# VectorE sums four experts in place of two, and the output projection is issued in halves

## What is computed

```python
y = jnp.moveaxis(ys, 0, 1) + D[None, None, :, None] * xh       # the scan's result, 384 wide
y = y.reshape(B, L, D_INNER) * jax.nn.silu(z)
h = y @ out_proj_w                                             # the output projection
v = _rmsnorm(h, norm2_w)
m = jax.nn.silu(v @ w_gate) * (v @ w_up) @ w_down
...
h1 = jnp.einsum('td,eid->tei', x2, w1)                         # 8 experts, x2 normed
h3 = jnp.einsum('td,eid->tei', x2, w3)
h = jax.nn.silu(h1) * h3
y = jnp.einsum('tei,edi,te->td', h, w2, cw)                    # cw: the routing weights
z = jax.nn.silu(x2 @ sw1.T) * (x2 @ sw3.T) @ sw2.T             # the shared expert
return (y + z).reshape(B, S, D)
```

## Time and profile before

| | us |
|---|---|
| median of 3 runs | 1014.93 (1013.69 to 1015.32) |
| profiled execution, its own time | 1016.41 |
| its span in the trace | 1014.4 |
| busy PE / PEld / DVE / ACT / POOL | 825.3 / 637.8 / 660.8 / 585.1 / 345.4 |
| share of the span | 81 / 63 / 65 / 58 / 34 % |

### The profile page before, as it was taken

The page is one execution under the profiler, slowest core; times in us unless marked ns, Lnnn a source line. Parts: engine busy times, 40 slices in busy tenths (PEclk is TensorE's granted clock), DMA queues, the critical chain, the costliest instruction groups (busy, mean ns, idle before and its releaser), DMA issues.

```text
span 1014.4 us, 22717 instructions
## 1 busy us (share of the span) xinstructions
PE 825.3 (81%) x7120; PEld 637.8 (63%) x7120; DVE 660.8 (65%) x1629; ACT 585.1 (58%) x1307; POOL 345.4 (34%) x508
## 2 busy tenths in 40 slices
PE   3363898888888888888888888888888888888867
PEld 2232676666667666666767666666766666676656
DVE  5565675757667685766768575766768576665524
ACT  3574565665656666665656566565666666565423
POOL 1222333343324344333433334332434433242402
PEclk9675999999999999999999999999999999999988
DMA  8200000000000000000000000000000000000000
GB/s 221 81 1 12 2 6 15 2 20 0 19 0 5 14 0 19 0 19 0 5 14 4 15 0 19 0 20 0 5 14 0 19 0 19 0 5 9 1 8 8
DMA packets 16466, 15.22 MB, mean 15 GB/s; under 512 B 6322, under 2 KB 15224, under 8 KB 16184
## 3 DMA queue, kind: packets, MB, share of 16 engines
q1 hardware_dynamic: 16440, 14.89, 5.5%
HBM read 10.69 MB, written 4.19 MB: 15 GB/s over the span
## 4 chain that ended last, share of the span: by engine, by line
PE 42%; DVE 23%; issue 16%; ACT 13%; POOL 3%; DVEq 1%; ACTq 1%; DMA 0%; POOLq 0%; SPq 0%
PE bank L1305 20%; DVE mr L1024 5%; DVE xa L966 4%; PE bank L1471 4%; PE bank L1513 3%; PE bank L1588 3%; PE bank L1537 3%; DVE w_raw L1188 2%; ACT L687 2%; ACT xk L651 2%; ACT L812 2%; ACT er L706 2%; DVE e_ge L1117 2%; POOL t L476 1%; PE bank L1450 1%
## 5 line engine op out<-in xcount | busy, mean ns | idle before, releaser
L1024 DVE SCALAR_TENSOR_TENSOR mr<-er,gm 128x512 f32<-128x512 f32 x192 | 129.2, 702 | 58.1 <-ACT er L706 57.7
L540 POOL TENSOR_TENSOR w_raw<-w_raw 128x384 f32<-128x384 f32 x96 | 99.2, 1034 | 145.9 <-ACT w_raw L767 143.6
L778 ACT ACTIVATE sg<-bank 128x256 f32<-128x256 f32 x144 | 55.3, 384 | 136.2 <-PE bank L1305 135.9
L1588 PE MATMUL bank<-w2t,w_raw 128*128 128x192 f32 x576 | 116.4, 329 | 7.4 <-ACT w_raw L767 7.4
L706 ACT ACTIVATE er<-bank 128x512 f32<-128x512 f32 x192 | 104.3, 597 | 30.4 <-PE bank L1450 29.9
L1471 PE MATMUL bank<-mr,xd 128*32 128x128 f32 x1536 | 90.9, 288 | 28.0 <-DVE mr L1024 26.6
L966 DVE SCALAR_TENSOR_TENSOR xa<-xr,cw_,xa 128x256 f32<-128x256 f32 x192 | 101.4, 536 | 4.4 <-ACT xa L617 0.4
L1305 PE MATMUL bank<-x_h,w_hi 128*128 128x256 f16 x288 | 79.9, 277 | 29.6 <-DVE w_raw L1188 27.5
L1188 DVE TENSOR_TENSOR w_raw<-sg,bank 128x256 f32<-128x256 f32 x144 | 60.3, 420 | 61.5 <-ACT sg L778 56.3
L1588 PEld LDWEIGHTS bank<-w2t,w_raw 128*128 128x128 f32 x576 | 90.5, 190 | 13.3 <-ACT w_raw L767 9.6
L737 ACT ACTIVATE sg<-bank 128x256 f32<-128x256 f32 x96 | 36.9, 384 | 105.2 <-PE bank L1305 104.8
(11 more groups left out here) (233 smaller groups left out, 2160.4 us busy)
## 6 DMA issues: line engine op xcount, KB each, us to landing
out<-w_raw SPq DMA_DIRECT2D x16, 192.0 KB, 2.0
w_raw<-weights SPq DMA_DIRECT2D x1, 1924.0 KB, 9.6
wt_raw<-weights SPq DMA_DIRECT2D x2, 962.0 KB, 14.9
pos<-position SPq DMA_DIRECT2D x16, 96.0 KB, 2.8
tok<-tokens SPq DMA_DIRECT2D x16, 70.0 KB
sums<-lj SPq DMA_DIRECT2D x16, 64.0 KB, 2.2
ri<-sums SPq DMA_DIRECT2D x64, 12.0 KB
w2t<-w SPq DMA_DIRECT2D x1, 864.0 KB, 19.7
```

Of the source, the lines that this page charges most:

```text
L540: pool.tensor_tensor(acc[:], acc[:], wt_out[:, e % NWT], ALU.add).then_inc(acc_done, 1)
L778: act.activation(sg[:, e % 2, :], p_pair[e % 2][:, 0:NB * Q], ACT.Silu).then_inc(sx_ready, 1)
L1024: ve.scalar_tensor_tensor(mr[:, r % NER], er[:, r % NER], 1.0, gm[:, b, :].unsqueeze(1).to_broadcast([128, HG, Q]), ALU.min, ALU.mult)\
L1588: ins = pe.matmul(p_out[(e + 1) % 2][:, b * D:(b + 1) * D], hh[:, e % NHH, b * Q:(b + 1) * Q], w2t[:, e, :], start=True, stop=True)
```

## The change

1. `NP` becomes 5 and `ND = NX - NP` is 4. ScalarE no longer weighs experts 5 and 6, GpSimd no longer adds them, VectorE's `weighed_sum` takes 5, 6, 7 and 8. The sum of expert 5 stands ahead of the product `hh` of expert 8 in VectorE's queue, the others behind it. TensorE's `down(7)` and `down(8)` wait for `out_sum`, no longer for `weighed`.
2. `project_out` is called once for each batch row; the exponents of unit 2 are issued between the two calls and those of unit 3 behind the second. In `scan` they are left out. The waits for `y_ready` are split likewise.
3. ScalarE's `mixed` comes ahead of the Exp of unit 3, not of unit 2.

```diff
-        NP = NX - 2
+        NP = NX - 4
+        ND = NX - NP
...
-                    for out_ in {2: (0,), 8: (5, 6)}.get(e, (e - 3,) if e > 3 else ()):
+                    for out_ in {2: (0,), 8: ()}.get(e, (e - 3,) if e > 3 else ()):
...
-                    scan(f, 0, {} if b is None else {2: lambda: mixed(b), 4: lambda: mixed_norm(b)})
+                    scan(f, 0, {} if b is None else {3: lambda: mixed(b), 4: lambda: mixed_norm(b)})
...
                 for e in range(NX):
+                    if e == NX - 1:
+                        weighed_sum(c, NP)
                     ve.wait_ge(sx_ready, c * NX + e + 1)
...
-                for e in range(NP, NX):
+                for e in range(NP + 1, NX):
                     weighed_sum(c, e)
...
-                    ve.wait_ge(out_sum, c * 2 + e - NP)
+                    ve.wait_ge(out_sum, c * ND + e - NP)
...
-                        if b * NQ + q + 2 < NR:
+                        if 3 < b * NQ + q + 2 < NR:
                             exponents(c, b * NQ + q + 2)
...
-            def project_out(c):
-                if not later(c):
-                    pe.wait_ge(in_late, 96)
-                    pe.wait_ge(dx_ready, 2)
-                pe.wait_ge(y_ready[0], c + 1)
-                pe.wait_ge(y_ready[1], c + 1)
-                if later(c):
-
-                    pe.wait_ge(out_sum, c * 2 - 1)
-                for b in range(NB):
-                    for k in range(DI // 128):
-                        ins = pe.matmul(p_out[0][:, b * D:(b + 1) * D], y[:, b, k, :], wo[:, k, :],
-                                        start=(k == 0), stop=(k == DI // 128 - 1))
-                ins.then_inc(m_out, 1)
+            def project_out(c, b):
+                if b == 0:
+                    if not later(c):
+                        pe.wait_ge(in_late, 96)
+                        pe.wait_ge(dx_ready, 2)
+                    if later(c):
+
+                        pe.wait_ge(out_sum, c * ND - 1)
+                pe.wait_ge(y_ready[b], c + 1)
+                for k in range(DI // 128):
+                    ins = pe.matmul(p_out[0][:, b * D:(b + 1) * D], y[:, b, k, :], wo[:, k, :],
+                                    start=(k == 0), stop=(k == DI // 128 - 1))
+                if b == NB - 1:
+                    ins.then_inc(m_out, 1)
...
-                        pe.wait_ge(weighed, c * NP + e - 1)
+                        if e - 2 < NP:
+                            pe.wait_ge(weighed, c * NP + e - 1)
+                        else:
+                            pe.wait_ge(out_sum, c * ND + e - 1 - NP)
...
-                    project_out(b)
+                    project_out(b, 0)
+                if f is not None:
+                    exponents(f, 2)
+                if b is not None:
+                    project_out(b, 1)
+                if f is not None:
+                    exponents(f, 3)
```

More of the change, by code:

```diff
@@ L382, in store @@
             def store(c):
-                sp.wait_ge(out_sum, c * 2 + 2)
+                sp.wait_ge(out_sum, c * ND + ND)
                 settle(sp)
@@ L1519, in turn_v @@
                 if later(c):
-                    pe.wait_ge(out_sum, c * 2)
+                    pe.wait_ge(out_sum, c * ND)
                 transpose_channels(p_out[1], vn, vt_done)
```

## The result

| | before | after |
|---|---|---|
| median | 1015.12 us (4 runs, 1013.69 to 1015.45) | 999.73 us (4 runs, 998.91 to 1004.04) |
| profiled execution, its span | 1016.41, 1014.4 | 999.18, 997.4 |
| mean granted TensorE clock | 0.962 | 0.959 |
| level pass (whole pass at granted clock 1.00) | 57.95 | 56.80 |

The changed kernel takes 0.986 of the time before, with an interval of 0.983 to 0.989: **15.4 us less**. The forecast was 1001.7 us, with a range of 993.3 to 1007.0.

What follows compares the result with a forecast made beforehand. No engine was taken as full: waits bound the kernel, at the boundary ScalarE's chain. 14 x 0.83 = 11.6, + 1.0 + 0.9 - 0.3 = 13.2 us off 1016.41, less 1.48 to the median: 1001.7 us, range 993.3 to 1007.

Steps and rivals of the forecast that it cites:

- Exponents 0, 1.09 us earlier: At the boundary between two bodies: without ScalarE's four weighings, TensorE starts exponents 0 1.09 us earlier, between 0.81 and 1.25.
- both legs nearly even: Ahead of exponents 0: TensorE, through VectorE's sums and `down(8)`, is free 0.1 us after ScalarE's `ecx`.
- VectorE's three steps: Ahead of `down(8)`: sum of expert 5 (0.76 us), `hh` of expert 8 (0.42), sum of expert 6 (0.76).
- the loop's branch: On TensorE, between `down(8)` and exponents 0: taken as 0.05 us, with bounds of nothing and 0.28.
- The projection in halves, 0.26 us: Exponents 2 ahead of the projection's second half makes the projection end 0.26 us later, counted from exponents 0.
- GpSimd in the way: In the scan: `decayed` starts 0.11 us ahead of `mr` of unit 3 and holds it until 0.55 us behind its end.
- the other outcome: Rival at `mr` of unit 3: VectorE starts first, GpSimd is held; 0.59 us more per boundary, 993.4 us; chance 0.15.
- A boundary, 0.83 us: Net gain at each of 14 boundaries: 1.09 us less 0.26; the rest of the pass moves as a block.
- The first projection, 0.3 us lost: At b = 0, with no experts ahead, only the new order acts: 0.3 us lost.
- the 0.97 us that I used of them: In the scan, `t1` can start 0.97 us after `state_read`, a distance read from rows of the kernel before.
- The ends, 1.0 and 0.9 us: Gains from VectorE's sums: 1.0 us at the last chunk's projection, 0.9 at the end of the kernel.
- my 13.2: The whole predicted gain in us: 11.6 for 14 boundaries, plus 1.0 and 0.9, less 0.3.

Runs made afterwards that it cites:

- e3: The changed kernel with GpSimd's copy `keep` put ahead of `decayed`; median 990.84 us, ratio 0.9784 to the kernel before.
- e4: The changed kernel with VectorE's `t1` of the first batch row moved behind `mr` of unit 3; median 984.99 us, ratio 0.9715 to the kernel before.
- e9: e11 with GpSimd's copy of h also put ahead of `decayed`, as in e3; median 980.38 us, ratio 0.9654 to the kernel before.
- e2: The kernel before with only the new order (projection in halves, exponents 2 and 3 and squares moved), sums unchanged; median 1016.98 us, ratio 1.0035.
- e10: The kernel before with 15 unread matmuls per pass in the second batch row's scan; median 1012.06 us, ratio 0.9971 to the kernel before.
- e6: e4 with 15 unread matmuls per pass in the second batch row's scan; median 975.60 us, ratio 0.9611 to the kernel before.
- e7: The changed kernel with 15 unread matmuls per pass in the second batch row's scan; median 993.98 us, ratio 0.9796 to the kernel before.
- e11: e5 with `t1` moved behind `mr` of unit 3, in the old order; median 988.11 us, ratio 0.9736 to the kernel before.
- e1: The kernel before with only the sums changed (VectorE takes four experts), projection and order as before; median 1008.03 us, ratio 0.9942.
- e8: The changed kernel with the sum of expert 5 made twice by VectorE, first into an unused tile; 1015.24 us in one run.
- e5: e1 with 15 unread matmuls per pass in the second batch row's scan; median 988.99 us, ratio 0.9753 to the kernel before.

## Why the prediction was right, step by step

**Exponents 0, 1.09 us earlier (0.81 to 1.25): measured 1.24.** The mechanism held: four weighings gone, both legs nearly even, a new short wait of `down(8)`. Two terms were mis-sized. I gave VectorE's three steps 0.76 + 0.42 + 0.76 = 1.94 us; they took 1.73, because instructions follow each other sooner than their durations say: `hh` starts at 439.02, takes 0.41, and the next sum starts at 439.35, 0.33 behind it. And for the loop's branch I took 0.05: exponents 0 starts 0.06 behind `ecx` (0.05 before), with no more room for a branch. The "about 108 ns" of the Trainium skill ("Advanced Engine Details and Errata", Control Flow Timing) is not seen exposed here. Whether `down(8)` or the wait for `ecx` covers it, the trace doesn't tell: the last weight load of `down(8)` ends at 440.76, and the next starts at 440.91.

**The projection in halves, 0.26 us: measured 0.20.** `junk` came 2.99 us behind exponents 0 (3.06 predicted), `state_read` 3.59 (3.62), `t1` 0.97 behind that (0.97).

**GpSimd in the way: as predicted.** `decayed` at `junk` + 1.89, `mr` of unit 3 5.04 us behind exponents 0 (5.06 predicted), 1.23 us long, ending 0.55 behind `decayed`. It was a near thing, 0.16 us by the trace (0.11 predicted), and e3 and e4 show the other outcome at the price that I had put on it. The Trainium skill ("SBUF — State Buffer", Who interferes with whom) has the one that is issued first keep the ports for its whole length. The rows agree in both directions: in e9 `mr` starts first (437.53), and then GpSimd's copy takes 1.37 us, not 0.51. It ends at 439.17, 0.36 behind the end of the second of two `mr` (438.81), so it was held over both, the second of which started after it.

**A boundary, 0.83 us: measured 1.15 per level pass.** It is 1.24 - 0.19 = 1.05 at the boundary and 0.10 more in the experts, at `hh` of expert 2. That last piece comes with the sums and not with the order (it isn't in e2); which of its three waits makes it stays open.

**The first projection, 0.3 us lost: 0.2 seen.** The first pass gained 4.3 us. Of that 3.1 are the two falls of the clock in the pass of before, on the projection (3.53 us, twice 1.14 after) and behind the scan: in e10 that pass has neither and takes 57.35 and not 60.46. (That the projection has no fall in e10 is not the work of the fills, since e6, e7 and e11 have them and the fall.) The other 57.35 - 56.18 = 1.17 are the gain at the boundary at its end less the cost of the new order at its start. That cost e1 shows, which has the old order and no fall in this pass either: 56.18 - 56.01 = 0.17 us. I had taken from that pass and had not looked at its clock; the 0.97 us that I used of them came out all the same.

**The ends, 1.0 and 0.9 us.** The last pass, e10 first (level clock, with fills) and after second:

```profile
909.36:958.82 49.46, 43.79 (x378) 33.32 (x378) 27.49 (x71) 24.63 (x58) 16.26 (x19) 1.00 0.02 5
```

```profile
898.65:947.49 48.84, 42.24 (x364) 32.02 (x363) 29.01 (x74) 23.51 (x54) 14.21 (x17) 1.00 0.02 5
```

That is 0.62 us, where the sum has 1.0 less the 0.26 of the order, 0.74; the remaining 0.57 of the 1.19 are again a fall in the pass of before (50.03, granted clock 0.97). The end of the kernel gave 1.0, predicted 0.9, at the same mean clock in both (0.85).

**What was missed: the clock.** The sum took both kernels at the same clock. At level clock the effect is 14 x 1.15 + 0.6 + 1.0 + 0.3 (ahead of the first projection) = 18.0 us, and e10 against e7 measures 18.1. That the two agree to 0.1 us is luck in part: e7 has a fall of 1.6 us on its first projection and e10 has none, and e10 comes to that projection 1.4 us later (98.27 against 96.89). The 18.1 are 4.9 more than my 13.2, and 14 x (1.15 - 0.83) = 4.5 of it is the boundary's term. The falls of before that are gone gave 2.4 + 3.1 + 0.6 = 6.1 us and those in five passes of after took 7.2: net 1.1 us lost in the two profiled executions (18.0 - 1.1 = 16.9, measured 17.0). The median shows 15.4: the profiled execution of before lay 1.3 us above its median and that of after 0.55 below its own, and the executions differ in their mean clock (after: 0.955 to 0.959, 998.91 to 1004.04 us). So the step of the sum that was mis-sized is the boundary, 0.83 us for 1.15, and the clock was left out. The two errors have opposite signs, and that the forecast lies only 2 us from the median (4 from the profiled execution, 1003.2 against 999.18) is luck. The range had no room for the second by reason: e1, with a pass 0.24 us shorter, is 8.3 us slower.

**What stays open.** Why the clock falls in one pass and not in the next, when the 6 us ahead of it are alike, no run shows. It isn't random: in e1 nine passes in a row have a fall, in e8 every second one from the second to the fourteenth. Shown is that TensorE's clock falls behind a thin stretch, and that filling the stretch removes these falls (e1 to e5, e4 to e6, after to e7, before to e10).

## What to carry to other kernels

Where a change shortens a wait by moving work to an idle engine, compute what is late next, leg by leg, and cost a chain of VectorE's by the distance from start to start, not by durations. Compare variants by passes at the same granted clock as well as by the median: here a variant with the shorter pass had the longer time, and in that variant (e1) a few matmuls of no use in TensorE's thin stretch were worth more than the change itself, while they brought 5.75 us in the changed kernel and 3.1 in the one before. Before a product of two SBUF operands on VectorE, look at what GpSimd starts within a few tenths of a us: who is first decided 0.55 us per pass, and one instruction moved behind it gave 1.13 in the new order and nothing in the old (e11).

## What the runs showed of the hardware

- TensorE's granted clock falls to 0.50, the 1.2 GHz level, behind a stretch in which it was busy for 4.01 of 6.00 us with no wait over 0.78 us, in some passes and not in others; in the loop each fall costs 0.7 to 1.6 us over all runs. With 15 small matmuls (2.1 us) put into that scan there are none behind it (e5, e6, e7, e9, e10, e11); the one fall that e6, e7 and e11 keep is on the first projection.
- VectorE's `mr`, with both tensors in SBUF, and GpSimd's `decayed` or copy hold each other until the one that started first is done: `mr` takes 1.23 us for 0.68, GpSimd's copy 1.37 for 0.51 (e9, held over two `mr`).
- VectorE's sums, with one operand in PSUM, ran beside GpSimd's `xw` without getting longer (before: four in 1.52 us beside it; after: two in 0.74 without it).
- `hh`, an instruction of 0.41 us on VectorE, is followed by the next 0.33 us behind its start.
